# The first four expert blocks load their first weights by number from DRAM; order chosen anew, 22 first blocks

## The chip, the cores and the metric

One core of one Trainium2 chip runs one fused kernel. The metric is device time in microseconds (us), the median of the runs; less is better. Matmuls and transposes run on PE (TensorE), elementwise work on DVE (VectorE), ACT (ScalarE) and POOL (GpSimd). Loads and stores are issued by SP (SyncE), scattered and accumulating ones by POOL.

## What is computed

Two transformer layers over x of 8 batches x 256 rows x 256. Layer 0: layer norm, attention with 16 query and 4 key heads of 128 (causal softmax), then a mixture of 8 experts (2 chosen for each token) and a shared expert, computed densely. Layer 1: layer norm, linear attention, then a mixture of 16 experts with 4 chosen for each token. The part that the change touches is the last one, cut to what matters:

```python
t = xf * rsqrt(mean(xf * xf) + EPS) * norm_w            # norm_w scales the 256 input columns
vals, idx = top_k(t @ gate_w.T + gate_b, 4)
G = softmax(vals) scattered to [tokens, 16]
h = einsum('mh,eoh->emo', t, w1) + b1[:, None, :]       # w1: 16 experts, 512 x 256
a, b = minimum(h[..., ::2], 7), clip(h[..., 1::2], -7, 7)
act = a * sigmoid(1.702 * a) * (b + 1.0)
y = einsum('emi,edi->emd', act, w2) + b2[:, None, :]
return x + einsum('me,emd->md', G, y)
```

## The kernel before

**The blocks.** The tokens of layer 1 are sent, each to its four experts' lists in DRAM (`xsD`), by an indirect DMA of POOL (`f_send`, L1897). The lists are then worked off in 79 blocks of 128 rows of one expert. A table (`bi`, written by the steps `n_mm` to `n_bi`, L1739) gives each block its expert's number and its place in the lists. It is made twice: once from the first `PART` = 5 batches, for the first `FIRST` = 21 blocks, and again when all eight batches are sent, for the other 58.

**The steps of a block n.** `xb(n)` (SP, L801 to L802) loads the 128 rows. `x_t(n)` (PE, L1065, two transposes) and `x_out(n)` (ACT, L1348, one copy of 128x256) bring them into `XT`. `w_in(n)` (ACT, L1339 to L1341) reads the expert's number and copies its first weights, two pieces of 128x512, out of `W1`, where all 16 experts' weights lie, into one of the two places of `WS`, scaling by `nw` (norm_w) on the way. `h_mm(n)` (PE, L1076, 16 matmul records) multiplies; `e_a`, `e_b` (DVE, L1757, L1764), `e_tanh` (ACT, L1354), `e_g`, `e_act` (DVE, L1772, L1777) follow; `w2x(n)` (SP, L810 to L811) loads the second weights by the expert's number; `y_mm(n)` (PE, L1085), `y_out` (DVE, L1785) and `y_add` (POOL, L1926, accumulating scatter) end the block. The results of `h_mm` stand in banks 2 and 3 in turn, until `e_b` has read them.

**Where `W1` lies.** `W1` is the whole of `RA`, 16 places of 1024 columns (512 KB each), and attention uses the same memory until its end: its q, k and v weights, its output weights, the keys, values and transposed inputs. `w12(i)` (SP, L828) fills the 16 places in three steps, as attention lets go of them: i = 0 places 4, 5, 10 and 12, once batch 6 has ended and the last k and v products are done; i = 1 five places after the last `q_mm`; i = 2 the last seven (3.5 MB) after `wo(127)`, attention's last matmul. Every `w_in` waits for all of it. `WS`, `W2`, `XT` lie in `RB`, on attention's other tiles.

**The order.** Each engine runs its instructions in program order, and that order is written out by a planner (`lay_out`, `Plan`), before the kernel is built. It holds a cost for each step (`ENGINE`), a time to landing for each load (`LANDING`), and chains of steps, each chain with an allowance (`KV` ... `TURN`): at each turn it takes the step with the smallest sum of start time and allowance. Steps that could run on an idle engine but are of less hurry (the first blocks: `FILL`) have a larger allowance. SP's waits stand in the same order: a load behind a wait isn't issued before the wait ends. Behind the last of the 21 blocks the order is a fixed loop.

**Batch 7 after attention.** When `wo(127)` is done, `res(0,7)` (DVE, L1688 to L1690), the norm (L1438 to L1466), `f_mul`, `f_add` (L695, L700), `f_t` (PE, L911), `f_ht` (ACT, L1280), `s_mm` (PE, L946), `f_sig` (ACT, L1313), the choice of experts, 16 rounds of `d_mm` (PE, L962), `d_tanh` (ACT, L1301) and `d_act` (DVE, L1543 to L1545) and `d_y` (PE, L984) follow each other, then linear attention (from L1111), routing, 8 `f_send`, `f_gain`, `f_x` (POOL, L1884, L1889) and `store(7)` (SP, L832). Only then come the loads of the 22nd block and what follows.

## Time and profile before

| | us |
|---|---|
| median of 3 runs | 1042.82 (1041.34 to 1048.06) |
| the profiled execution | 1043.59 |
| its span (first to last instruction) | 1041.7 |
| PE busy | 970.5 (93% of the span) |
| DVE busy | 722.6 (69%) |
| ACT busy | 671.3 (64%) |
| POOL busy | 427.1 (41%) |
| mean granted PE clock | 0.974 of full |

An engine that is busy for most of the span is near to being the bound, but the share is a mean over stages that differ. The granted clock is that of PE: 1.0 is the upper of its two levels, 2.4 GHz, and 0.5 the lower, 1.2 GHz. The DMA share is the mean busy share of the core's 16 DMA engines.

### The profile page before, as it was taken

To read this page: it belongs to the slowest core of one execution; us is meant where nothing else is said; L and a number is where in the kernel's file an instruction comes from. 1 tells how busy PE (TensorE), PEld (TensorE's weight loads), DVE (VectorE), ACT (ScalarE), POOL (GpSimd) and SP (SyncE) were. 2 spreads that over 40 slices of the span, in tenths; PEclk is the share of its full clock that TensorE was granted. 3 is DMA by queue.
4 is the path that set the end of the run, shared out by engine and by line. 5 is a ranking of instruction groups with operands and counts; after the bars stand their busy time and mean duration, and the time that the engine had idled before them with its cause. 6 is when DMAs were issued, how large, how long until landed. Compare 5 with 4: busy or idle time off the path is not lost.

```text
span 1041.7 us, 20507 instructions
## 1 busy us (share of the span) xinstructions
PE 970.5 (93%) x6020; PEld 820.9 (79%) x6020; DVE 722.6 (69%) x2545; ACT 671.3 (64%) x1944; POOL 427.1 (41%) x450
## 2 busy tenths in 40 slices
PE   6999999999999999999999999996888799999990
PEld 4669888887988888888888888884677689999980
DVE  3564775777677678677867867776867668888870
ACT  2657786687677767757866776782735456676650
POOL 3322431342362353154236225224064555665673
PEclk9999999999999999999999999998999899999995
DMA  9928993994789210020012004057177699998954
GB/s 307 307 80 301 376 371 113 375 377 164 278 293 376 96 62 1 18 88 31 1 62 73 2 1 165 3 183 264 52 188 169 188 247 217 225 226 215 225 133 81
DMA packets 93725, 180.53 MB, mean 173 GB/s; under 512 B 9949, under 2 KB 29085, under 8 KB 92717
## 3 DMA queue, kind: packets, MB, share of 16 engines
q1 hardware_dynamic: 73467, 148.55, 43.1%
q0 software_dynamic: 18800, 30.30, 12.9%
q8 instruction: 48, 0.79, 0.3%
q10 hardware_dynamic: 1346, 0.36, 0.2%
q14 instruction: 64, 0.52, 0.2%
HBM read 77.71 MB, written 107.99 MB: 178 GB/s over the span
## 4 chain that ended last, share of the span: by engine, by line
PE 86%; DVE 4%; issue 3%; ACT 2%; DMA 2%; POOL 1%; SPq 0%; ACTq 0%; DVEq 0%; POOLq 0%; another core or an unknown queue 0%
PE bank L1076 12%; PE bank L1040 11%; PE bank L1012 10%; PE bank L1085 6%; PE bank L1030 5%; PE bank L1002 5%; PE bank L991 4%; PE bank L962 3%; PE bank L868 3%; PE bank L1031 3%; PE bank L1001 3%; PE bank L1021 3%; PE bank L877 3%; PE bank L946 2%; PE bank L984 2%
## 5 line engine op out<-in xcount | busy, mean ns | idle before, releaser
L1076 PE MATMUL bank<-RB 128*128 128x128 f32 x1264 | 157.8, 279 | 6.1 <-issue 3.8
L1076 PEld LDWEIGHTS bank<-RB 128*128 128x128 f32 x1264 | 150.6, 195 | 9.6 <-issue 4.6
L1871 POOL TENSOR_TENSOR RB<-RB 128x512 f32<-128x512 f32 x64 | 67.6, 1056 | 203.1 <-DVE RB L1650 203.1
L1040 PE MATMUL bank<-RA,RB 128*128 128x256 f32 x512 | 133.7, 383 | 1.1 <-DVE X L1690 0.8
L1341 ACT ACTIVATE RB<-RA,nw 128x512 f32 x158 | 105.5, 715 | 37.2 <-issue 16.5
L1012 PE MATMUL bank<-RA 128*128 128x256 f32 x512 | 121.2, 380 | 0.0
L1012 PEld LDWEIGHTS bank<-RA 128*128 128x128 f32 x512 | 95.2, 190 | 15.0 <-issue 2.9
L1040 PEld LDWEIGHTS bank<-RA,RB 128*128 128x128 f32 x512 | 91.0, 190 | 15.5 <-issue 4.7
L1847 POOL TENSOR_TENSOR qs<-qs,half 128x4 f32<-128x4 f32 x64 | 64.9, 1014 | 93.1 <-DVE qs L1659 79.6
L1085 PE MATMUL bank<-RB,BC 128*128 128x256 f32 x316 | 83.2, 387 | 3.3 <-DVE BC L1777 2.3
L1242 ACT ACTIVATE RB<-bank 128x256 f32<-128x256 f32 x128 | 48.7, 381 | 57.9 <-PE bank L1031 52.8
L1897 POOL DMA_INDIRECT xsD<-SC,pu x64 | 63.7, 996 | 46.7 <-DVE pu L1586 31.2
L1650 DVE COPY RB<-bank 128x512 f32<-128x512 f32 x64 | 44.2, 691 | 49.2 <-PE bank L1012 47.5
L1030 PE MATMUL bank<-RB,RA 128*128 128x256 f32 x256 | 77.0, 382 | 0.0
L1002 PE MATMUL bank<-RA 128*128 128x256 f32 x256 | 76.5, 380 | 0.0
L1223 ACT ACTIVATE RB<-bank 128x384 f32<-128x384 f32 x128 | 62.6, 491 | 20.7 <-PE bank L991 18.7
L1670 DVE CUSTOM_DVE_ANT_0 RB<-bank,cb,qs 128x128 f32<-128x128 f32 x128 | 44.1, 345 | 34.4 <-PE bank L1002 27.5
L1757 DVE TENSOR_SCALAR RB<-bank,b 128x128 f32<-128x128 f32 x158 | 48.0, 345 | 28.3 <-PE bank L1076 20.4
L1216 ACT ACTIVATE RB<-RB,sm 128x128 f32<-128x128 f32 x128 | 51.0, 398 | 20.6 <-DVE sm L1671 19.8
L991 PE MATMUL bank<-ident,RB 128*128 128x128 f32 x384 | 63.0, 273 | 1.1 <-ACT RB L1242 1.1
L1217 ACT ACTIVATE RB<-RB,sm 128x256 f32<-128x256 f32 x128 | 63.9, 500 | 0.0
L1236 ACT ACTIVATE RB<-RB,sm 128x256 f32<-128x256 f32 x128 | 63.9, 499 | 0.0
(251 smaller groups left out, 2387.3 us busy)
## 6 DMA issues: line engine op xcount, KB each, us to landing
xsD<-BC SPq DMA_DIRECT2D x17, 4232.0 KB, 33.0
RB<-in_w2b SPq DMA_DIRECT2D x79, 256.0 KB
RB<-xsD SPq DMA_DIRECT2D x62, 264.5 KB
BC<-modD SPq DMA_DIRECT2D x16, 512.0 KB, 4.2
X<-xsD SPq DMA_DIRECT2D x17, 264.5 KB, 3.4
RA<-in_w SPq DMA_DIRECT2D x2, 2048.0 KB, 8.0
RA<-in_w SPq DMA_DIRECT2D x6, 512.0 KB, 11.5
RA<-in_L_attn_Wq SPq DMA_DIRECT2D x1, 2048.0 KB, 13.8
```

What stands on the lines that cost most here:

```text
L991: m = pe.transpose(psum("p_t", u)[:, n * 128:n * 128 + 128], P[:, u % 4, n * 128:n * 128 + 128], ident[:, :])
L1002: pe.matmul(ps[:, 128:384], q[:, 128:256], k[:, 0:256], start=True, stop=True).then_inc(mine("scores", u), 1)
L1012: m = pe.matmul(psum("q_mm", p)[:, t * 256:t * 256 + 256], hT[:, b % 2, c, t * 128:t * 128 + 128], Wq[:, c, h * 128:h * 128 + 256], start= ...
L1030: pe.matmul(psum("pv", u)[:, 0:256], v[:, 0, :], PT[:, u % 2, 0:256], start=True, stop=False, skip_group_check=True)
L1040: m = pe.matmul(bank[5][:, t * 256:t * 256 + 256], OT[:, u % 2, t * 128:t * 128 + 128], Wo[:, h, :], start=(h == 0 and t == 0), stop=(h == ...
L1076: m = pe.matmul(ps[:, 128 * j:128 * j + 128], WS[:, n % 2, c, 128 * j:128 * j + 128], XT[:, n % 2, c * 128:c * 128 + 128], start=(c == 0), ...
L1085: m = pe.matmul(ps[:, 0:256], AB[:, n % 3, c * 128:c * 128 + 128], W2[:, n % 4, c, :], start=(c == 0), stop=(c == 1))
L1217: act.activation(P[:, u % 4, 128:384], P[:, u % 4, 128:384], ACT.Exp, bias=s[:, 3:4], scale=-1.0, accum_out=s[:, 5:6]).then_inc(mine("s_ex ...
L1236: act.activation(P[:, u % 4, 128:384], P[:, u % 4, 128:384], ACT.Copy, scale=s[:, 7:8]).then_inc(mine("p_norm", u), 1)
L1341: m = act.activation(WS[:, n % 2, c, :], W1[:, bass.ds(r, 1), c, :].rearrange("p a n -> p (a n)"), ACT.Copy, scale=nw[:, c:c + 1])
L1847: pool.tensor_tensor(dst, src, half[:, 0:n], ALU.pow).then_inc(sem, 1)
L1871: pool.tensor_tensor(sq, qrow, qrow, ALU.mult).then_inc(mine("q_sq", p), 1)
```

## The change

The first four blocks don't copy their weights out of `W1` any more. `w1x(n)`, n = 0 to 3, reads the expert's number of block n from the table and loads that expert's 512 KB straight from DRAM into place `PLACES[n]` (4, 5, 10, 12) of `W1`. It does so at the point at which `w12(0)` filled these places; `w12(0)` is gone. `h_mm(n)` of these four reads its weights there and waits for `w1x(n)`, not for `w_in(n)`. As these weights aren't scaled by `nw`, `x_out(n)` scales the rows instead, in two activations of 128x128. Behind `h_mm(n)`, `w12x(n)` loads the place's own expert into it (512 KB each). `w_in(n)` is there from n = 4 on and waits for `w12x(3)` beside what it waited for. `FIRST` goes from 21 to 22, so the fixed loop has 57 blocks. The planner gets costs and landing times for the new steps (5 us and 6 us), five of its ten allowances change, and chains now carry their batch, so that batch 5's chains are given 1 us more once attention has ended. With that the order of all engines is chosen anew.

```diff
-FIRST, PART = 21, 5
+FIRST, PART = 22, 5
+PLACES = 4, 5, 10, 12
+DURING, BEHIND = {5: 0, 6: 0}, {5: 1, 6: 0, 7: 0}
...
-        "SP": "clear 2.0 w12 1.0 xb 1.2 w2x 1.2 store .1 bc .1 mod_store .1 acc_zero 2.8 zrow_store 2.0",
+        "SP": "w1x .1 w12x .1 clear 2.0 w12 1.0 xb 1.2 w2x 1.2 store .1 bc .1 mod_store .1 acc_zero 2.8 zrow_store 2.0",
...
-HOP, LANDING = 0.2, {"bc": 5.0, "mod_store": 4.0, "clear": 14.0, "w12": 11.0, "xb": 3.2, "w2x": 3.5, "y_add": 4.0, "f_send": 3.0, "store": 4.0}
+HOP, LANDING = 0.2, {"w1x": 5.0, "w12x": 6.0, "bc": 5.0, "mod_store": 4.0, "clear": 14.0, "w12": 11.0, "xb": 3.2, "w2x": 3.5, "y_add": 4.0, "f_send": 3.0, "store": 4.0}
...
+    def allowance(self, c):
+        late, of = c[2].get("late", c[0]), c[4]
+        return late + (BEHIND if ("wo", NU - 1) in self.end else DURING).get(of, 0.0)
...
-    KV, QUERY, FIRSTS, SHARED, DENSE, LINEAR, LATE, UNIT, FILL, TURN = 0.04, 0, 0.1, 0.02, 0.0, 0.06, 0.1, 0.1, 0.19, -0.09
+    KV, QUERY, FIRSTS, SHARED, DENSE, LINEAR, LATE, UNIT, FILL, TURN = -0.08, 0, 0.1, 0.07, 0.0, -0.02, 0.1, 0.1, 0.24, 0.11
...
     def last_weights():
-        yield do("w12", 0, by=48, aside=True, after=[("pv", NU - 17), ("k_mm", NB - 1, 1), ("v_mm", NB - 1, 0), ("v_mm", NB - 1, 1)])
...
-        yield do("h_mm", n, bank=2 + n % 2, first=True, after=[("w_in", n)] + [("h_mm", n - 1)] * (n > 0))
+        yield do("h_mm", n, bank=2 + n % 2, first=True, after=[("w1x", n), ("wo", NU - 1)] * (n < len(PLACES)) + [("w_in", n)] * (n >= len(PLACES)) + [("h_mm", n - 1)] * (n > 0))
...
     def weights_in():
-        for n in range(FIRST):
-            yield do("w_in", n, aside=True, after=[("w12", 2), ("n_bi", 0)] + [("h_mm", n - 2)] * (n >= 2))
+        for n in range(len(PLACES), FIRST):
+            yield do("w_in", n, aside=True, after=[("w12", 2), ("w12x", len(PLACES) - 1), ("n_bi", 0)] + [("h_mm", n - 2)] * (n >= len(PLACES) + 2))
+
+    def first_weights():
+        for n in range(len(PLACES)):
+            yield do("w1x", n, slot=n, by=16, aside=True, after=[("n_bi", 0), ("pv", NU - 17), ("k_mm", NB - 1, 1), ("v_mm", NB - 1, 0), ("v_mm", NB - 1, 1)])
+
+    def weights_behind():
+        for n in range(len(PLACES)):
+            yield do("w12x", n, by=16, aside=True, after=[("h_mm", n)])
...
+            def w1x(n):
+
+                on.wait_ge(*done("n_bi", 0))
+                on.wait_ge(*done("pv", NU - 17))
+                for t in range(2):
+                    on.wait_ge(*done("k_mm", NB - 1, t))
+                    on.wait_ge(*done("v_mm", NB - 1, t))
+                r = sp.value_load(table(0, n), min_val=0, max_val=15)
+                sp.dma_start(W1[:, PLACES[n]:PLACES[n] + 1, :, :].rearrange("p e c n -> p (e c n)"),
+                             I["w1"].rearrange("p (e n) -> p e n", e=16)[:, bass.ds(r, 1), :].rearrange("p e n -> p (e n)")).then_inc(mine("w1x", n), 16)
+
+            def w12x(n):
+
+                on.wait_ge(*done("h_mm", n))
+                e = PLACES[n]
+                sp.dma_start(W1[:, e:e + 1, :, :].rearrange("p e c n -> p (e c n)"), I["w1"][:, 1024 * e:1024 * e + 1024]).then_inc(mine("w12x", n), 16)
...
-                on.wait_ge(*done("w_in", n))
+                if n < len(PLACES):
+                    w = W1[:, PLACES[n], :, :]
+                    on.wait_ge(*done("w1x", n))
+                else:
+                    w = WS[:, n % 2, :, :]
+                    on.wait_ge(*done("w_in", n))
...
-                act.activation(XT[:, n % 2, :], psum("x_out", n)[:, 0:256], ACT.Copy).then_inc(mine("x_out", n), 1)
+                if n < len(PLACES):
+                    on.wait_ge(L["small1"], 128)
+                    for c in range(2):
+                        m = act.activation(XT[:, n % 2, 128 * c:128 * c + 128], psum("x_out", n)[:, 128 * c:128 * c + 128], ACT.Copy, scale=nw[:, c:c + 1])
+                    m.then_inc(mine("x_out", n), 1)
+                else:
+                    act.activation(XT[:, n % 2, :], psum("x_out", n)[:, 0:256], ACT.Copy).then_inc(mine("x_out", n), 1)
```

## Rows read from the trace of the kernel before

**Rows 1.** The page: PE's busy share in 40 slices, in tenths.

```profile
PE   6999999999999999999999999996888799999990
```

**Rows 2.** Windows: length, busy time of each engine (instructions), granted clock, DMA share, GB/s.

```profile
core 0: us, PE busy (x) PEld busy (x) DVE busy (x) ACT busy (x) POOL busy (x), PEclk, DMA share, GB/s
...
600.00:700.00 100.00, 98.78 (x618) 83.62 (x616) 71.37 (x275) 73.22 (x226) 33.47 (x37) 1.00 0.27 91
711.00:729.00 18.00, 8.09 (x25) 4.74 (x24) 12.63 (x29) 2.48 (x6) 8.38 (x9) 0.72 0.95 341
...
711.00:845.00 134.00, 105.17 (x673) 85.79 (x672) 97.02 (x329) 63.58 (x149) 63.85 (x68) 0.90 0.66 182
```

**Rows 3.** Windows: two at the lower clock, one before; columns as in rows 2.

```profile
718.20:728.20 10.00, 3.99 (x9) 2.54 (x10) 7.10 (x15) 1.26 (x3) 2.42 (x3) 0.50 0.99 366
...
824.00:834.00 10.00, 6.21 (x22) 4.72 (x21) 4.02 (x12) 0.75 (x3) 7.93 (x8) 0.50 0.85 270
...
640.00:676.00 36.00, 35.67 (x212) 30.74 (x213) 28.11 (x122) 25.36 (x80) 12.12 (x12) 1.00 0.16 60
```

**Rows 4.** Timeline of PE: start, us, operation, idle before it and what ended it.

```profile
723.53 1.11 PE L911 MATMUL bank<-ident,SC 128*128 128x128 f32 x4 [8.38 <-DVE SC L700]
725.33 4.16 PE L946 MATMUL bank<-RB,SC 128*128 128x360 f32 x8 [0.69 <-ACT SC L1280]
729.42 2.05 PE L1076 MATMUL bank<-RB 128*128 128x128 f32 x16
```

**Rows 5.** Timeline of PE: `s_mm` of an earlier batch, at the upper clock.

```profile
570.89 2.58 PE L946 MATMUL bank<-RB,SC 128*128 128x360 f32 x8
```

**Rows 6.** Timeline of ACT: the first weight copies and their neighbours.

```profile
728.03 1.33 ACT L1341 ACTIVATE RB<-RA,nw 128x512 f32 x2 [2.27 <-DMA RA<-in_w]
729.27 0.43 ACT L1313 ACTIVATE rt<-bank 128x8 f32<-128x8 f32 x2
...
735.37 0.70 ACT L1301 ACTIVATE SC<-bank,gh 128x176 f32<-128x176 f32 x2
```

**Rows 7.** Timeline of SP's queue: loads of weights and rows.

```profile
634.76 42.18 SPq L828 DMA_DIRECT2D RA<-in_w  x5
...
712.77 2.06 SPq L828 DMA_DIRECT2D RA<-in_w  x4
716.62 4.12 SPq L811 DMA_DIRECT2D RB<-in_w2b  x4
```

**Rows 8.** DMA from 711 to 731.5 us; and L828's time to landing.

```profile
DMA packets 2008, 7.01 MB, mean 342 GB/s; under 512 B 251, under 2 KB 500, under 8 KB 1880
...
DMA to landing us min/median/max: 6.0/9.8/12.9
```

**Rows 9.** Timeline of PE: `h_mm` among batch 7's `d_mm`, then `d_mm` without.

```profile
737.32 0.46 PE L962 MATMUL bank<-RB,SC 128*128 128x352 bf16 x2
...
740.02 0.46 PE L962 MATMUL bank<-RB,SC 128*128 128x352 bf16 x2
...
744.66 0.47 PE L962 MATMUL bank<-RB,SC 128*128 128x352 bf16 x2 [0.17 <-DVE SC L1545]
...
747.04 0.47 PE L962 MATMUL bank<-RB,SC 128*128 128x352 bf16 x2 [0.95 <-DVE SC L1545]
```

**Rows 10.** The end of the transition: loads for the loop, and its first `h_mm`.

```profile
838.03 8.53 SPq L802 DMA_DIRECT2D RB<-xsD  x8
...
844.71 2.02 PE L1076 MATMUL bank<-RB 128*128 128x128 f32 x16 [0.35 <-ACT RB L1348]
```

**Rows 11.** Chain of waits in the loop: start, us, what.

```profile
873.58 1.79 PE bank L1076 x16
...
876.45 1.79 PE bank L1076 x16
```

**Rows 12.** `e_a` of a block on the timeline, and the table's writing.

```profile
734.18 0.61 DVE L1757 TENSOR_SCALAR RB<-bank,b 128x128 f32<-128x128 f32 x2 [0.88 <-issue]
...
L1739 DVE TENSOR_TENSOR bi<-bank,SC x2: 228/228/229, 644.2 to 823.9; 1x80 int32<-1x80 f32 x2
```

More of the change, by code:

```diff
@@ L111, in add, with chain @@
         self.order.append(k)
-    def chain(self, late, steps):
-        self.chains.append([late, steps, next(steps), 0.0])
+    def chain(self, late, steps, of=None):
+        self.chains.append([late, steps, next(steps), 0.0, of])
+    def allowance(self, c):
+        late, of = c[2].get("late", c[0]), c[4]
+        return late + (BEHIND if ("wo", NU - 1) in self.end else DURING).get(of, 0.0)
     def begin(self, c):
-        late, steps, ask, ready = c
+        late, steps, ask, ready, _ = c
         t = ready
@@ L146, in run @@
                 t, bank = self.begin(c)
-                late = c[2].get("late", c[0])
+                late = self.allowance(c)
                 if t is not None and (best is None or t + late < best[0]):
@@ L295, in unit @@
             yield do("res", 0, b, bank=5, last=True, after=[("bc", 0, b)])
-            p.chain(FIRSTS, ffn0(b))
+            p.chain(FIRSTS, ffn0(b), b)
     def ffn0(b):
@@ L307, in ffn0 @@
         for i in range(2):
-            p.chain(SHARED, shared(b, i))
+            p.chain(SHARED, shared(b, i), b)
         yield do("f_top", 0, b, after=[("f_sig", b, 0), ("f_sig", b, 1)])
@@ L313, in ffn0 @@
             for r in range(2):
-                p.chain(DENSE, dense(b, i, r))
+                p.chain(DENSE, dense(b, i, r), b)
             for h in range(2):
-                p.chain(DENSE, turned(b, i, h))
+                p.chain(DENSE, turned(b, i, h), b)
     def shared(b, i):
@@ L329, in shared @@
                 yield do("bc", 0, b + 3, slot=b % 3, by=16, after=[("s_x", b, 0)], aside=True)
-            p.chain(LINEAR, lin_attn(b))
+            p.chain(LINEAR, lin_attn(b), b)
     def dense(b, i, r):
@@ L366, in lin_attn @@
         yield do("res", 1, b, bank=f0, last=True)
-        p.chain(LATE, ffn1(b))
+        p.chain(LATE, ffn1(b), b)
     def ffn1(b):
@@ L391, in ffn1 @@
         yield do("f_w", 1, b)
-        p.chain(LATE, offsets(b))
+        p.chain(LATE, offsets(b), b)
         yield do("f_pos", 1, b, bank=bk, last=True, after=[("f_rank", 1, b)])
@@ L466, in lay_out @@
     p.chain(LATE, last_weights())
-    for steps in (weights_in(), weights_out(), block(0)):
+    for steps in (first_weights(), weights_behind(), weights_in(), weights_out(), block(0)):
         p.chain(FILL, steps)
@@ L811, in w2x @@
                 sp.dma_start(W2[:, n % 4, :, :].rearrange("p c n -> p (c n)"), I["w2b"][bass.ds(r, 1), :, :].rearrange("a p n -> p (a n)")).then_inc(mine("w2x", n), 16)
-            def w12(i):
-                if i == 0:
-                    on.wait_ge(*done("pv", NU - 17))
-                    for t in range(2):
-                        on.wait_ge(*done("k_mm", NB - 1, t))
-                        on.wait_ge(*done("v_mm", NB - 1, t))
-                    parts = ((4, 6), (10, 11), (12, 13))
-                elif i == 1:
+            def w1x(n):
[11 more added lines that the diff above has]
+                sp.dma_start(W1[:, e:e + 1, :, :].rearrange("p e c n -> p (e c n)"), I["w1"][:, 1024 * e:1024 * e + 1024]).then_inc(mine("w12x", n), 16)
+            def w12(i):
+                if i == 1:
                     on.wait_ge(*done("q_mm", NU // 2 - 1))
@@ L834, in _ @@
             run = {"mod_store": mod_store, "bc": bc, "acc_zero": acc_zero, "zrow_store": zrow_store,
-                   "clear": clear, "xb": xb, "w12": w12, "w2x": w2x, "store": store}
+                   "clear": clear, "xb": xb, "w1x": w1x, "w12x": w12x, "w12": w12, "w2x": w2x, "store": store}
             for stage, *key in plan.order:
@@ L1075, in h_mm @@
                     for c in range(2):
-                        m = pe.matmul(ps[:, 128 * j:128 * j + 128], WS[:, n % 2, c, 128 * j:128 * j + 128], XT[:, n % 2, c * 128:c * 128 + 128], start=(c == 0), stop=(c == 1))
+                        m = pe.matmul(ps[:, 128 * j:128 * j + 128], w[:, c, 128 * j:128 * j + 128], XT[:, n % 2, c * 128:c * 128 + 128], start=(c == 0), stop=(c == 1))
                 m.then_inc(mine("h_mm", n), 1)
@@ L1335, in w_in @@
                 on.wait_ge(*done("w12", 2))
+                on.wait_ge(*done("w12x", len(PLACES) - 1))
                 on.wait_ge(L["small1"], 128)
-                if n >= 2:
+                if n >= len(PLACES) + 2:
                     on.wait_ge(*done("h_mm", n - 2))
```

## The prediction, made before the changed kernel was run

> **What bounds the kernel now.** I read the page's slices first: PE is 9 tenths or more busy in all but a few slices, and the dip lies between slice 28 and slice 34, some 700 to 860 us [rows 1]. Then the windows: in the last 100 us of attention PE is busy for 98.78 of them, so little can be won there; from 711 us, when attention's last matmul runs, to 845 us, when the loop over the last 58 blocks takes over, PE is busy for 105.2 of 134 us and its granted clock is 0.90 [rows 2]. The transition is the place where something is to be had: 28.8 us of idle PE, and four stretches with the clock at 0.50, the lower of its two levels, of which the first and the last are shown (10 us each; the two between them have about 3 us each) [rows 3].
>
> The largest hole is the first. In 711 to 729 us PE works 8.1 us [rows 2]: it waits 8.4 us for batch 7's norm and shift on DVE, and the `f_t` and `s_mm` that follow run at the lower clock; `s_mm` takes 4.16 us [rows 4], against 2.58 us for the same 8 records of an earlier batch [rows 5]. The rows of the first blocks are there, but their weights are not: the last seven places of `W1` are only issued from 712.8 us, when attention is over [rows 7], and ACT's first weight copy waits for them until 728.0 us [rows 6]. The first `h_mm` is at 729.4 us [rows 4].
>
> The end of the transition is set by a chain, not by the amount of work: batch 7 has to go through its experts, linear attention and routing, and be sent, before the first rows of the loop can be loaded, at 838.0 us; the loop's first `h_mm` is at 844.7 us [rows 10]. From there PE is the bound, a block each 2.87 us (876.45 - 873.58) [rows 11].
>
> **The change part by part.** I make the sum against the profiled execution, 1043.6 us, which is 0.8 us above the median of the runs.
>
> *Loads ahead.* The table is written at 644.2 us [rows 12]. In place of three loads by place SP issues four by number. Its queue issued five `w12` loads in 42 us [rows 7] and the DMA engines are 0.16 busy there [rows 3], so the table reads are covered by idle time: a load by number takes 4.12 / 4 = 1.0 us of SP, one by place 2.06 / 4 = 0.5 us [rows 7], 2.6 us more in all if the cover were gone. Bytes are the same. A load of this kind lands 6.0 to 12.9 us after its issue [rows 8]; `h_mm(0)` comes tens of us later. Nothing.
>
> *The four `h_mm`.* They can now run from 711.6 us on, in the hole: 4 x 1.79 us (the length of one) [rows 11] = 7.2 us of PE work leaves the stretch after 729 us. What that is worth there is not 7.2 us but what batch 7's chain gains. Two rounds of `d_mm` with an `h_mm` between them start 2.70 us apart (740.02 - 737.32), two rounds without 2.38 us (747.04 - 744.66) [rows 9]. Three `h_mm` stood in such places. Bounds: 3 x 0.3 = 1 us by these rows, 3 x 1.79 = 5.4 us if each held the chain for its whole length. ACT helps: of the six weight copies between 728 and 744 us four go, each 1.33 us, and one of them stands right in front of `f_sig` [rows 6]. I take 2.4 us, nearer the lower end.
>
> *The clock.* In the first stretch at the lower level PE has 3.99 us of work [rows 3], all of it on batch 7's chain. If the `h_mm` keep PE at work in the hole, and the clock stays up, half of that goes: 2.0 us. Bounds 0 and 2.0; I take 2.0, as the hole of 8.4 us is what lies ahead of the fall, and three or four `h_mm` leave no part of it longer than some 3 us.
>
> *DVE's share.* `e_a` and `e_b` are 0.6 us each [rows 12]. DVE has 18 - 12.63 = 5.4 us idle in the window [rows 2], but not always where these steps come. If they push in front of batch 7's norm, the chain loses up to the 2.4 us of two blocks; if they fit into idle time, nothing. I take 1.0 us of loss. The second activation of `x_out` (some 0.3 us a block, from the 0.43 us pair at 729.27 [rows 6]) falls into ACT's idle 15.5 us of the 18 [rows 2].
>
> *One block more in the transition.* It leaves the loop: 2.87 us less, if PE has the room, and 28.8 us of idle time say so. It costs up to 2.87 us if its row load or its bank comes so late that it delays the loop's first block. I take 2.9 us of gain.
>
> *The places' own weights.* `w12x(n)` adds 4 x 512 KB = 2.1 MB behind `h_mm(n)`. Between 711 and 731.5 us the queues move 7.01 MB at 342 GB/s [rows 8], with a DMA share of 0.95 to 0.99 [rows 2, 3]: there is no room beside them, so `w12x(3)` lands up to 2.1 MB / 342 GB/s = 6.1 us after that work, near 737.6 us. `w_in(4)` can't start before. With four blocks ahead this is covered: the y half of these blocks and batch 7's experts are to be done until then. In the kernel before, the fifth `h_mm` came far later still, after the first four blocks' y half. What stands behind `w_in(4)` on ACT isn't covered; that is the first rival. The Trainium skill says in "DMA: Bandwidth & Descriptors", section "Issuing engines are not separate DMA queues", that transfers issued by SP, ACT and POOL all run on the same 16 DMA engines and interleave. By this rule the sends and the second weights delay `w12x` wherever it is issued. The shares of 0.95 and more agree. If it were not so, the nearest row would let it land 6.0 us after its issue, near 733 us; the sum stays the same in both cases, the first rival's chance doesn't.
>
> *The order.* New allowances move the steps everywhere. In attention PE is 0.99 busy [rows 2], and I cost it at 0, with 2 us either way. In the transition the last stretch of low clock has 6.2 us of PE's work in it [rows 3], 3.1 us to be lost or won, and the two short ones, of some 3 us each, up to 3.2 us more, by chance of order. I cost it at 0, with 5 us either way.
>
> Sum: 1043.6 - 2.4 - 2.0 + 1.0 - 2.9 = 1037.3 us for a profiled execution, and 0.8 less, **1036.5 us**, as a median.
>
> **The rivals.**
>
> *The wait moves to `w_in(4)` (slower).* ACT runs in order. If the planner, which lets `w12x` land 6 us after its issue, writes `w_in(4)` in front of batch 7's `f_sig` or first `d_tanh`, these stand behind a load that lands at 737.6 us. `f_sig` would go from 729.3 us to 737.6 + 1.33 = 738.9 us, 9.6 us later; the first `d_tanh`, from 735.4 us, 3.5 us later [rows 6]. With the first, the gains in clock and rounds are gone too: 1043.6 - 2.9 + 9.6 = 1050.3, as a median 1049.5 us. It decides once the stall is over 2.9 us with the other gains gone, or over 6.3 us with them. For it: ACT stood 2.27 us in front of just such a copy [rows 6]. Against it: four `h_mm` and their e steps are ready before, so the copy is hardly written early.
>
> *Only the extra block counts.* The chain of batch 7 doesn't move, since its own latencies and DVE set it and what goes in the first hole comes back in another: 1043.6 - 2.9 - 0.8 = 1039.9 us. For it: PE has idle time in all parts of the transition. Against: its `s_mm` at half clock is on the chain itself.
>
> *All of it counts.* The four `h_mm` were fully in the chain's way: 7.2 + 2.0 + 2.9 = 12.1 us, 1030.7 us. For it: PE's idle time after 729 us is short pieces, behind which each `h_mm` pushes the next. Against it: rows 9.
>
> *The order costs.* The hole closes, but the new order opens others, with another fall of the clock: 5 us plus the forecast's gain lost in part, 1045 us.
>
> **How the numbers follow.** Forecast 0.42 (own range 1034 to 1039), all of it 0.19, only the block 0.18, the order costs 0.12, the wait moved 0.09. 1036.5 us is that of the likeliest. The range for 8 in 10 goes from 1030 (all of it, less what attention may give) to 1046 (order costs); the wait moved and the tails stay out. Faster by over 1% means under 1032.4 us: all of it with luck and the low tail, 0.23. Slower by over 1% means over 1053.2 us: the moved wait at its worst, 0.04. The rest, 0.73, is within 1%, about what a measurement of this kernel can tell from no change.
>
> **What would show it.** Right: `h_mm` records (L1076 before) from some 713 us after the start of the span on, three or four before `s_mm`; `s_mm` in 2.6 us; clock 1.0 in the first window; the loop's first `h_mm` 3 to 4 us earlier and 57 blocks behind it. Wrong: ACT idle in front of `w_in(4)` and released by a DMA; `f_t` of batch 7 later than 12 us after attention's last `wo`; `s_mm` still above 4 us; a long wait in front of the loop's first rows.

## The result, and the profile after

The changed kernel took 1051.09 us, median of 12 runs (1046.93 to 1055.72), beside 1044.54 us for the kernel before on the same chip (12 runs, 1041.34 to 1048.06): 1.0065 times as long, 95% interval 1.0049 to 1.008. That is 0.65% slower, within 1%, and 5 us above the range given (1030 to 1046 us). The same kernel was measured twice more, always beside the kernel before. On chip 11 it took **0.9914** (0.9895 to 0.9932), on chip 7 **1.006** (1.0037 to 1.0082). So there are two results. The later runs were made on five chips, one session on each, and fall into two kinds, which I call kinds of chip; whether it is the chip or the session that decides isn't told apart by them:

| | kind A (chips 9, 11) | kind B (the first chip, whose number isn't known, and chips 7, 0, 13; the first may be one of these) |
|---|---|---|
| the kernel before, us | 1040.35, 1039.95 | 1044.54, 1044.66, 1043.29, 1042.34 |
| the changed kernel, ratio | 0.9914 | 1.0065, 1.006 |

The forecast, 1036.5 of 1042.82 us, is a ratio of 0.994. Kind A comes 0.3% below it, kind B 1.2 to 1.3% above it. The spans split like this (attention's end is the end of the last `wo`; all times read from the timeline):

| us | before, first chip | after, first chip | after, chip 11 |
|---|---|---|---|
| to attention's end | 712.7 | 715.1 | 705.9 |
| from there to batch 7's first `f_send` | 107.6 | 105.6 | 105.1 |
| from there to the loop's first `h_mm` | 24.4 | 33.4 | 26.6 |
| the loop and the end | 197.0 (58 blocks) | 195.7 (57) | 195.2 (57) |
| span | 1041.7 | 1049.8 | 1032.8 |

The two executions of the changed kernel are of one program, and differ in the first row and in the third, by 9.2 and 6.8 us. The middle of the transition, which the change was to shorten, is the same in both and 2.0 to 2.5 us shorter than before. The forecast had 6.3 us less for the profiled execution: 3.4 on batch 7's chain and 2.9 for the block. The first chip has 8.1 us more: 2.4 at attention's end, -2.0 on the chain, 9.0 at the loop's start and -1.3 in the loop.

Attention's last `wo` (L1068) in the two executions, first chip, then chip 11:

```profile
714.05 1.03 PE L1068 MATMUL bank<-RA,RB 128*128 128x256 f32 x4
```

```profile
704.90 1.03 PE L1068 MATMUL bank<-RA,RB 128*128 128x256 f32 x4
```

Windows of after, first chip; the first answers to the second row of [rows 2], the second to its third row:

```profile
core 0: us, PE busy (x) PEld busy (x) DVE busy (x) ACT busy (x) POOL busy (x), PEclk, DMA share, GB/s
...
715.10:731.00 15.90, 13.50 (x108) 12.94 (x108) 11.58 (x38) 4.69 (x13) 1.92 (x2) 1.00 0.95 368
715.10:854.10 139.00, 111.86 (x716) 92.25 (x715) 100.56 (x346) 61.80 (x148) 59.05 (x63) 0.89 0.64 178
822.00:854.00 32.00, 21.98 (x112) 18.07 (x111) 15.86 (x52) 9.07 (x19) 18.06 (x18) 0.73 0.67 179
```

The hole behind attention is filled: PE is busy for 13.5 of 15.9 us at clock 1.00, where it had 8.09 of 18 us at 0.72 [rows 2]. The transition as a whole is as idle as it was (27.1 us of 139, before 28.8 of 134), at 0.89 against 0.90. The last window shows where the idle time went: to the end, with the clock at 0.73.

PE's timeline there, which answers to [rows 4], and ACT's, which answers to [rows 6]:

```profile
714.92 1.95 PE L1109 MATMUL bank<-RB,RA 128*128 128x128 f32 x16
...
727.20 1.10 PE L1118 MATMUL bank<-RB,BC 128*128 128x256 f32 x4 [2.40 <-DMA RB<-in_w2b]
...
731.04 1.38 PE L974 MATMUL bank<-RB,SC 128*128 128x360 f32 x4
```

```profile
738.29 2.56 ACT L1375 ACTIVATE RB<-RA,nw 128x512 f32 x4 [0.59 <-issue]
740.96 0.70 ACT L1334 ACTIVATE SC<-bank,gh 128x176 f32<-128x176 f32 x2
```

`h_mm` (L1109) starts 0.2 us before attention's matmuls have drained. `s_mm` (L974) has its full clock (all 8 records in 2.59 us), but starts at 731.0, 16.0 us after attention's end, where it was 12.6 us (725.33 - 712.74): linear attention of batch 6 and four blocks' PE work stand before it, and a wait of 2.40 us of `y_mm(0)` (L1118) for its second weights. `w_in(4)` (L1375) does stand in front of the first `d_tanh` (L1334), for 2.56 us, but waits for no load.

The loop's start, SP and PE, which answers to [rows 10]:

```profile
845.69 0.34 SPq L828 DMA_DIRECT2D RB<-in_w2b  x1
846.07 0.43 SPq L860 DMA_DIRECT2D out<-X  x1
847.65 7.85 SPq L819 DMA_DIRECT2D RB<-xsD  x8
...
854.10 2.02 PE L1109 MATMUL bank<-RB 128*128 128x128 f32 x16 [0.35 <-ACT RB L1388]
```

`store(7)` (L860) waits behind `w2x(21)` (L828), and this for `y_mm(17)`, which is late. `f_x` of batch 7 had ended at 836.7 us, and the loop's rows could have been loaded from there.

### The profile page after: what moved, and what is told of

Same layout as the page of the kernel before. It is cut to its first block, busy times and chain, and to the rows that moved or that the text cites. A ratio compares the mean times of both kernels' runs of the same rounds, so it can differ in the third digit from the quotient of the medians.

```text
span 1049.8 us, 20509 instructions
## 1 busy us (share of the span) xinstructions
PE 974.0 (93%) x6020; PEld 823.9 (78%) x6020; DVE 722.2 (69%) x2545; ACT 670.0 (64%) x1940; POOL 426.5 (41%) x450
## 4 chain that ended last, share of the span: by engine, by line
PE 83%; DVE 4%; issue 3%; DMA 3%; ACT 2%; POOL 1%; another core or an unknown queue 1%; SPq 1%; DVEq 0%; ACTq 0%; POOLq 0%
PE bank L1109 11%; PE bank L1068 10%; PE bank L1040 10%; PE bank L1118 5%; PE bank L1030 5%; PE bank L1058 5%; PE bank L1019 4%; PE bank L990 3%; PE bank L1029 3%; PE bank L1059 3%; PE bank L896 3%; PE bank L1049 3%; PE bank L905 3%; PE bank L1012 2%; PE bank L974 2%
## 5 line engine op out<-in xcount | busy, mean ns | idle before, releaser
L1911 POOL TENSOR_TENSOR RB<-RB 128x512 f32<-128x512 f32 x64 | 66.9, 1046 | 237.5 <-DVE RB L1690 236.7
L1109 PE MATMUL bank<-RB 128*128 128x128 f32 x1200 | 151.3, 281 | 1.5 <-ACT RB L1388 1.3
L1109 PEld LDWEIGHTS bank<-RB 128*128 128x128 f32 x1200 | 145.0, 197 | 3.6 <-ACT RB L1388 1.7
L1068 PE MATMUL bank<-RA,RB 128*128 128x256 f32 x512 | 133.7, 384 | 3.0 <-ACT RB L1275 2.9
L1375 ACT ACTIVATE RB<-RA,nw 128x512 f32 x150 | 100.0, 714 | 56.9 <-issue 17.7
L1068 PEld LDWEIGHTS bank<-RA,RB 128*128 128x128 f32 x512 | 92.0, 191 | 16.9 <-ACT RB L1275 4.0
L1118 PE MATMUL bank<-RB,BC 128*128 128x256 f32 x316 | 84.3, 391 | 12.1 <-DVE BC L1817 7.3
L1118 PEld LDWEIGHTS bank<-RB,BC 128*128 128x128 f32 x316 | 55.1, 194 | 20.0 <-DVE BC L1817 9.8
L1334 ACT ACTIVATE SC<-bank,gh 128x176 f32<-128x176 f32 x128 | 49.3, 404 | 24.8 <-PE bank L990 21.5
```

The lines of the kernel that those rows point to most:

```text
L1068: m = pe.matmul(bank[5][:, t * 256:t * 256 + 256], OT[:, u % 2, t * 128:t * 128 + 128], Wo[:, h, :], start=(h == 0 and t == 0), stop=(h == ...
L1109: m = pe.matmul(ps[:, 128 * j:128 * j + 128], w[:, c, 128 * j:128 * j + 128], XT[:, n % 2, c * 128:c * 128 + 128], start=(c == 0), stop=(c ...
L1118: m = pe.matmul(ps[:, 0:256], AB[:, n % 3, c * 128:c * 128 + 128], W2[:, n % 4, c, :], start=(c == 0), stop=(c == 1))
L1375: m = act.activation(WS[:, n % 2, c, :], W1[:, bass.ds(r, 1), c, :].rearrange("p a n -> p (a n)"), ACT.Copy, scale=nw[:, c:c + 1])
L1911: pool.tensor_tensor(sq, qrow, qrow, ALU.mult).then_inc(mine("q_sq", p), 1)
```

## Late signals of PE: what sets the two kinds apart

On chips of kind B the timeline has waits whose releaser isn't seen: the profile calls it remote. In the changed kernel on the first chip each ends with a signal of PE (a semaphore counted up) that is on record 1.9 to 3.5 us behind the end of the last matmul that gives it. ACT in the changed kernel, first chip:

```profile
640.92 0.38 ACT L1275 ACTIVATE RB<-bank 128x256 f32<-128x256 f32 x1 [4.91 <-remote]
...
695.71 0.49 ACT L1256 ACTIVATE RB<-bank 128x384 f32<-128x384 f32 x1 [1.06 <-remote]
...
782.52 1.33 ACT L1375 ACTIVATE RB<-RA,nw 128x512 f32 x2 [3.53 <-remote]
...
835.84 1.33 ACT L1375 ACTIVATE RB<-RA,nw 128x512 f32 x2 [11.72 <-remote]
```

The same first and last instruction on chip 11:

```profile
637.65 0.39 ACT L1275 ACTIVATE RB<-bank 128x256 f32<-128x256 f32 x1 [3.05 <-PE bank L1059]
...
818.61 1.33 ACT L1375 ACTIVATE RB<-RA,nw 128x512 f32 x2 [4.11 <-PE bank L1118]
```

The eight profiles taken on chips 9 and 11, of seven kernels, have not one such wait. The other profiles all have them: the kernel before 2 or 4, 7.6 and 9.6 us in sum over the engines; the changed kernel 7 or 8, 30 to 32 us. In the changed kernel they stand at the same seven instructions on the first chip and on chip 7, five of them with the same length within 0.4 us (4.91 and 4.97 us for the first); with 21 blocks on chip 13 six of the seven come again (4.79 us). They end in POOL's bursts of eight sends or behind them, most within 2 us, the last at 835.8 us 5 us behind. In the changed kernel these are at 632 to 644 us (batch 4), 688.6 to 698.5 (batch 5), 771 to 782 (batch 6) and 820.7 to 830.7 (batch 7). The kernel before has the largest of its own there too, and the profile before showed it, though I didn't read it:

```profile
830.40 0.38 ACT L1348 ACTIVATE RB<-bank 128x256 f32<-128x256 f32 x1 [6.33 <-remote]
```

The trace's records of the semaphores say it without the waits. In the eight profiles of kind A all of PE's counts that can be set beside a matmul (1,265 in each) come within 0.02 us of its recorded end. In each of the twelve of kind B 10 to 24 come 0.5 us or more behind it, up to 4.1 and 4.6 us in the changed kernel and 6.3 us in the kernel with the sends moved (below). Except at the very end of some profiles, where counts before them are missing, DVE's are at most 0.06 us late on either kind.

What differs between the kernels is what a burst falls on. Before, batch 5's sends run from 706 to 715 us, across attention's end, where PE soon has little to do. The new order puts them inside attention (POOL, then PE, first chip):

```profile
688.59 1.06 POOL L1937 DMA_INDIRECT xsD<-SC,pu  x1 [2.68 <-DVE pu L1626]
...
697.57 0.96 POOL L1937 DMA_INDIRECT xsD<-SC,pu  x1 [0.31 <-issue]
```

```profile
694.71 1.13 PE L1068 MATMUL bank<-RA,RB 128*128 128x256 f32 x4 [0.56 <-ACT RB L1275]
...
698.28 0.55 PE L1019 MATMUL bank<-ident,RB 128*128 128x128 f32 x3 [1.11 <-issue]
...
701.50 2.07 PE L1068 MATMUL bank<-RA,RB 128*128 128x256 f32 x4 [2.37 <-ACT RB L1275]
```

```profile
692.60:699.50 6.90, 4.78 (x32) 3.43 (x30) 1.65 (x6) 3.44 (x11) 4.71 (x5) 1.00 0.57 221
699.50:706.30 6.80, 4.80 (x17) 3.75 (x18) 0.91 (x3) 4.08 (x12) 0.00 (x0) 0.50 0.05 17
```

PE, which is 0.99 busy in attention [rows 2], has three gaps within 7 us, 4.0 us in sum. Its granted clock falls to 0.50 at 699.5 us, at the start of the third gap (699.1 to 701.5 us), and stays there for 6.8 us; in the 6.9 us before, PE had worked 4.8. On chip 7 it was 13.7 us from 699.9 us. Laid record by record beside chip 11, the first chip is 2.7 us behind at 641.6 us, 3.5 at 694.7 and 9.1 at 706.5; then the lag stays within a microsecond or two until it grows again, from 10.7 us at 828.0 to 17.5 at 838.7, behind the last burst. Of the 17.0 us between the two executions some 14 are made in and behind bursts of sends: 1.4 at batch 4's, 5.6 at batch 5's, 6.8 at batch 7's.

## The experiments

Each number is a ratio to the kernel before on the same chip, with its 95% interval. Chip 9 first.

**The changed kernel with 21 first blocks.**

```diff
-FIRST, PART = 22, 5
+FIRST, PART = 21, 5
```

> The changed kernel with 21 first blocks in place of 22; all else (loads by number, new allowances) as in the changed one, the order chosen by the planner again. If the 22nd block is what costs (its steps stand in front of store(7) and of the loop's loads on SP), this comes out at or under the time of the kernel before, 1037 to 1045 us, and the loads of the loop start within 2 us of store(7)'s data, at 836 to 838 us. If the order or the loads by number cost, it stays at 1049 to 1053 us.

0.9919 (0.9898 to 0.994), 1032.79 of 1040.35 us, below both ranges that I expected. The forecast's ratio came in here, with all of the change but one block. Its mechanism didn't: attention ends at 707.1 us, which the forecast had at no gain, and the runs below show that batch 7's chain gains nothing from the loads. That the number fits on kind A is luck.

**The loads by number alone**: the changed kernel with 21 blocks, the old allowances and nothing for batch 5 behind attention.

```diff
-FIRST, PART = 22, 5
+FIRST, PART = 21, 5
...
-DURING, BEHIND = {5: 0, 6: 0}, {5: 1, 6: 0, 7: 0}
+DURING, BEHIND = {5: 0, 6: 0}, {5: 0, 6: 0, 7: 0}
...
-    ... = -0.08, 0, 0.1, 0.07, 0.0, -0.02, 0.1, 0.1, 0.24, 0.11
+    ... = 0.04, 0, 0.1, 0.02, 0.0, 0.06, 0.1, 0.1, 0.19, -0.09
```

> The loads by number alone: allowances as in the kernel before, 21 first blocks. If the loads by number do what the forecast says, 1038 to 1042 us (4 us less than before) with three or four h_mm in the first 16 us after attention. If they cost something themselves (2.1 MB more, w_in(4) in front of batch 7's d_tanh), 1046 to 1052 us.

1.0062 (1.0045 to 1.0079): slower by itself. Its PE timeline says why:

```profile
723.50 1.11 PE L939 MATMUL bank<-ident,SC 128*128 128x128 f32 x4 [4.12 <-DVE SC L717]
727.53 2.04 PE L1118 MATMUL bank<-RB,BC 128*128 128x256 f32 x4 [2.92 <-DMA RB<-in_w2b]
729.36 4.49 PE L974 MATMUL bank<-RB,SC 128*128 128x360 f32 x8
```

Three `h_mm` go into the hole, but the y half of block 0 now comes in front of `s_mm` and waits 2.92 us for its second weights, which are in the queues with the last 3.5 MB. `s_mm` runs at the lower clock as before, 4 us later, and attention's end to the first send is 113.1 us, not 107.6 (107.3 in the kernel before with 22 blocks, on the same chip).

**The new order alone**: the kernel before, with the new allowances and the 1 us of batch 5.

```diff
-    ... = 0.04, 0, 0.1, 0.02, 0.0, 0.06, 0.1, 0.1, 0.19, -0.09
+    ... = -0.08, 0, 0.1, 0.07, 0.0, -0.02, 0.1, 0.1, 0.24, 0.11
...
+        return late + (1.0 if of == 5 and ("wo", NU - 1) in self.end else 0.0)
```

> The new allowances alone (with batch 5's 1 us), weights loaded as in the kernel before, 21 first blocks. If the order is what costs (batch 6's linear attention is still to do when attention ends), 1048 to 1054 us, and attention's last matmul runs 2 us later than in the kernel before, near 714 us. If it doesn't, 1042 to 1047 us.

1.0002 (0.9987 to 1.0016), a little under both ranges. Neither part gains anything alone; together they gain 0.8%. Against the sum of the parts (+0.6 + 0.0) that is 1.4% for the pair. Where it comes from shows beside the first run (the first of batch 7's sends, and the loop's first `h_mm`), here:

```profile
810.66 1.00 POOL L1902 DMA_INDIRECT xsD<-SC,pu  x1 [0.59 <-DVE pu L1591]
...
845.52 2.02 PE L1081 MATMUL bank<-RB 128*128 128x128 f32 x16 [0.35 <-ACT RB L1353]
```

and with the loads by number (21 blocks, the same chip):

```profile
811.15 1.01 POOL L1937 DMA_INDIRECT xsD<-SC,pu  x1 [2.23 <-DVE pu L1626]
...
834.49 3.17 PE L1109 MATMUL bank<-RB 128*128 128x128 f32 x16
```

| us | new order alone | with the loads by number |
|---|---|---|
| attention's end | 706.3 | 707.1 |
| from there to the first send | 104.3 | 104.1 |
| from there to the loop's first `h_mm` | 34.9 | 23.3 |
| first blocks whose `h_mm` is still to do at the first send | 6 | 3 |

The order alone gains in attention and on batch 7's chain, and loses it again at the loop's start, where six of the first blocks are still to do. The loads by number give nothing on the chain; they let blocks run earlier and give 11.6 us at the loop's start. With 22 blocks on chip 11 it is the same: 105.0 and 105.1 us, then 37.7 and 26.6 us.

**22 first blocks alone**, in the kernel before.

```diff
-FIRST, PART = 21, 5
+FIRST, PART = 22, 5
```

> The kernel before with 22 first blocks and nothing else. If the 22nd block's steps in front of the loop's loads cost, 1046 to 1052 us; if the block fits into the transition's idle time, 1040 to 1043 us, 2.9 us less than with 21.

0.9978 (0.9962 to 0.9995), 2.4 us, where the sum had 2.9.

Then chip 11.

**The changed kernel itself, unedited, and once more with 21 blocks.**

> The changed kernel once more, beside its twin with 21 first blocks on one chip. The two have the same order on all engines up to the last first blocks (some 815 us), yet the profiles differ by 8 us at attention's end. If that is of the chip and of the single execution, attention ends here at 706 to 709 us and the ratio to the kernel before is 1.000 to 1.008; the stretch from batch 7's first f_send to the loop's first h_mm (33.4 us in the first profile) tells what the 22nd block costs by itself: still 31 us or more by the theory that the last first blocks are late, 24 to 27 us by the theory that the first profile was a bad execution. The latter gives 0.99 for the ratio.

> The changed kernel with 21 first blocks again, on the same chip as the one with 22. If 21 against 22 first blocks is the whole difference, 0.990 to 0.994 of the kernel before, as in the first measurement, with f_send to the loop's first h_mm in 23 to 24 us. If the first measurement was luck, 1.00.

0.9914 (0.9895 to 0.9932) and 0.9927 (0.991 to 0.9944). With the first two parts of the change the 22nd block adds too little to be told from nothing.

**`w2x(21)` moved behind `store(7)` and the loop's first rows.**

```diff
+    late = ("w2x", FIRST - 1)
+    p.order.remove(late)
+    p.order.insert(p.order.index(("w2x", FIRST)), late)
```

> The changed kernel, 22 first blocks, with one step moved on SP: w2x(21), which waits for y_mm(17), stands behind store(7) and the eight row loads of the loop, not in front of them. If SP's queue holds the loop, the loads start at f_x(7)'s end (836.7 us by the first profile, not 847.7) and the kernel gains 5 to 9 us against the changed one. If PE is late by itself, with the last first blocks' h_mm and y_mm still in front of the loop's, the loads start early but the kernel gains under 2 us.

0.9998 (0.9983 to 1.0013): 0.8% lost beside the changed kernel, where I had expected a gain either way. The store is issued 1.9 us earlier (826.32 us), but PE's order isn't changed, and there `y_mm(21)` stands before the loop's first `h_mm`:

```profile
841.27 2.05 PE L1121 MATMUL bank<-RB,BC 128*128 128x256 f32 x4 [9.44 <-DMA RB<-in_w2b]
```

The wait in front of the store is the cheaper of the two. The stretch from the first send to the loop's first `h_mm` is 34.2 us, not 26.6.

**The new order with the old weights and 22 blocks**: the kernel of the new order alone, with `FIRST` = 22.

> New allowances and 22 first blocks, weights loaded as in the kernel before (no loads by number). With 21 first blocks this order ran at 1.000 of the kernel before. If the 22nd block costs only where the fill is late, it costs here too, as the fill starts at 720 us: 1.004 to 1.010. If it is worth its 2.9 us as in the kernel before's order, 0.997.

1.0007 (0.9993 to 1.0022), neither of the two expected. The 22nd block gives 2.4 us in the old order and nothing in the new one.

Chip 7, kind B.

**The kernel before against itself, and the changed kernel for the third time.**

> The kernel before itself, timed against itself. If the ratio of the first measurement (1.0065) and of the second (0.9914) for the same changed kernel differ by the conditions of the chip, this one still has to give 1.000 within its interval, some 0.15% either way; a ratio off by more than 0.3% would say that the comparison itself is not as narrow as its interval. Its profile gives the milestones of the kernel before on this chip (on the first: attention's last matmul at 712.7 us, the loop's first h_mm at 844.7 us).

> The changed kernel for the third time. Theory A (the first measurement was made under conditions in which PE's signals come late while POOL sends, and those are rare): 0.991, as the second time. Theory B (it is a matter of the chip, and chips differ): anything between 0.991 and 1.007, and a profile that shows in which stretch it lies: attention's end at 706 or 715 us, the stretch from the last send to the loop's first h_mm 26 or 33 us. Theory C (pure chance of an execution): both values among the single times of this one run.

0.9991 (0.9979 to 1.0004) and 1.006 (1.0037 to 1.0082). The comparison is as narrow as it says, and the first result comes again with all its late signals. Theory C falls: of 6 single times here none is below 1047.5 us, of 6 on chip 11 none above 1034.6.

**`w12x` with a sixteenth of its bytes.** Fifteen sixteenths of each place's own weights are left out, so later blocks of these experts compute with wrong ones.

```diff
-sp.dma_start(W1[:, e:e + 1, :, :]..., I["w1"][:, 1024 * e:1024 * e + 1024])
+sp.dma_start(W1[:, e:e + 1, 0:1, 0:64]..., I["w1"][:, 1024 * e:1024 * e + 64])
```

> The changed kernel in its own order, but w12x loads 128x64 numbers a place, not 128x1024, so three of the four places keep the wrong expert's weights and their blocks' results are wrong: 2.0 MB less move in the first 20 us after attention. If the added bytes delay w2x(0) and w_in(4), as the working of the prediction had it (up to 6.1 us at w_in(4)), it is 1 to 3 us faster than the changed kernel beside it (0.997 to 0.999 of it). If they are covered, as the sum took it: the same, within 0.1%.

1.0049 (1.0028 to 1.007), 0.999 of the changed kernel beside it, with intervals that overlap. The medians are 2.6 us apart, the ratios 1.1 us: the added 2.1 MB cost 1 to 3 us or nothing.

**`w2x(0)` issued ahead of the last seven places.**

```diff
+    p.order.remove(("w2x", 0))
+    p.order.insert(p.order.index(("w12", 2)), ("w2x", 0))
```

> The changed kernel with one step of SP's queue moved: w2x(0) is issued ahead of the last seven places of W1 and not behind them, so that y_mm(0), which stood 2.4 us on PE in the profile of the changed kernel, finds its weights. If that wait is on batch 7's chain (f_t and s_mm are behind y_mm(0) on PE), attention's end to s_mm is 2 to 2.4 us shorter than in the changed kernel's run of the same job (17.5 us on the chip of the second measurement) and the time 0.998 of it. If DVE's norm sets s_mm anyway, it is the same.

1.0071 (1.005 to 1.0092), no gain. `s_mm` does start 13.3 us after attention's end and not 17.5, but the first send comes 108.6 us after it, not 105.7. An earlier `s_mm` was given back on the way; where, I haven't traced.

Chip 0, kind B.

**Batch 5's sends behind attention.**

```diff
+    sends = [k for k in p.order if k[0] == "f_send" and k[2] == 5]
+    for k in sends:
+        p.order.remove(k)
+    at = p.order.index(("f_add", 0, NB - 1)) + 1
+    p.order[at:at] = sends
```

> The changed kernel with one group moved: POOL issues the eight f_send of batch 5 behind f_add(0,7), some 10 us after attention's last matmul, and not inside attention's last 20 us. Chips differ so far: on two of them (before at 1040 us) the changed kernel takes 0.991, on one and in the first measurement (before at 1044.6 us) 1.006, and there PE's granted clock falls at 700 us, behind these sends, for 7 to 14 us. Theory A (on such a chip PE's signals come late during a burst of sends, the idle time that this makes lets the clock fall, and the changed order has put one burst where PE is otherwise busy without a gap): on such a chip attention's end comes back from 713 to 718 us towards 707 to 710 us and the ratio falls from 1.006 to 0.998 to 1.002; on the other kind of chip 0.991 to 0.995, as nothing is to be won there. Theory B (the sends have no part in it): the ratio stays 1.006 or 0.991, and a fall of the clock near 700 us stays on the first kind.

1.0047 (1.0033 to 1.006), above the 0.998 to 1.002 of theory A and below the 1.006 of theory B. The mechanism shows as theory A has it, the gain mostly doesn't. Attention ends at 707.9 us, the late signal at 695 and the fall of the clock at 700 us are gone, and a late signal stands behind the sends' new place (POOL, then DVE and ACT):

```profile
711.88 1.06 POOL L1942 DMA_INDIRECT xsD<-SC,pu  x1 [0.17 <-issue]
...
720.84 0.96 POOL L1942 DMA_INDIRECT xsD<-SC,pu  x1 [0.30 <-issue]
```

```profile
723.36 0.56 DVE L1850 TENSOR_TENSOR SC<-bank,mask 128x384 f32<-128x384 f32 x1 [5.99 <-remote]
```

```profile
723.42 0.60 ACT L1318 ACTIVATE SC<-bank 128x512 f32<-128x512 f32 x1 [5.19 <-remote]
```

Nearly all of the 7.2 us won (715.1 to 707.9) is lost again: the way from attention's end to the first send is 112.5 us, not 105.6. The counts for which DVE and ACT wait there come 6.3 and 6.0 us behind the ends of their matmuls. ACT's is that of batch 7's own `f_t`, so the late signal now stands on its chain.

**The new order alone, and the loads alone, once more.**

> The kernel of the allowances alone, once more. It has the changed order up to attention's end, its sends of batch 5 with it, and not the loads by number. Theory A: on a chip of the slower kind it loses what the changed kernel loses before attention's end, some 5 to 8 us, and goes from 1.000 to 1.005 or more; on the other kind 1.000 again. Theory B: 1.000 on either.

> The kernel of the loads by number alone, once more. It has the order of before up to attention's end, with the sends of batch 5 at 706 to 715 us, in the hole. Theory A: on a chip of the slower kind it loses no more than the kernel before, so 1.006 again, as on the other kind. Theory B (the loads by number themselves make the changed kernel's loss on such a chip): over 1.012.

1.0143 (1.0116 to 1.017) and 1.011 (1.0087 to 1.0132). The new order, worth 1.0002 on kind A, costs 1.4% on kind B: attention ends at 716.5 us, and the first send to the loop is 41.1 us. Windows of its last stretch of attention, to the last `wo`: chip 0, then chip 9.

```profile
694.00:716.50 22.50, 18.91 (x84) 13.88 (x82) 5.10 (x15) 10.16 (x27) 5.74 (x6) 0.77 0.23 84
```

```profile
692.00:706.30 14.30, 13.31 (x82) 10.52 (x80) 5.23 (x15) 8.97 (x25) 6.09 (x7) 1.00 0.36 139
```

84 and 82 matmuls in 22.5 and in 14.3 us. With the sends moved, and with the changed kernel on the first chip, for comparison:

```profile
695.00:708.00 13.00, 12.02 (x75) 9.76 (x74) 4.55 (x14) 8.16 (x23) 2.89 (x3) 1.00 0.20 62
```

```profile
695.70:715.00 19.30, 15.52 (x81) 12.20 (x80) 5.26 (x15) 10.38 (x29) 5.12 (x6) 0.82 0.26 89
```

The loads alone I expected at 1.006 on either kind; that was wrong by 0.5%. This kernel has two late signals that chip 9 doesn't have, 7.03 us on ACT at 716.7 and 6.67 us on DVE at 764.8 us, behind batch 5's and 6's sends. So the order is the larger part of the loss on kind B, not the whole.

Chip 13, kind B.

**Batches 5 to 7 send 256 bytes a row, not 2116.** They go to a memory of their own, so the rows of these batches are missing from the lists.

```diff
-pool.indirect_dma_start(xsD[:, :], ..., route(1)["src"][:, i, 0:ROW], None)
+pool.indirect_dma_start(xsD[:, :] if b < 5 else xsE[:, :], ..., route(1)["src"][:, i, 0:ROW if b < 5 else 64], None)
```

> The changed kernel, in its own order, but the sends of batches 5 to 7 write 256 bytes a row and not 2116, into a memory of their own, so the rows of these batches don't reach the lists and the result of their blocks is wrong; number and place of the sends are the same. If late signals of PE come from the bytes of the sends, the waits of an unseen releaser behind batches 5, 6 and 7 (1.1, 2 to 3.5 and 3 to 12 us in the changed kernel) are gone on a chip of the slower kind, the clock doesn't fall at 700 us and attention ends at 706 to 709 us; that behind batch 4 (4.9 us) stays. If they come from the number of packets or of signals, all stay. On a chip of the other kind there are none to begin with, and it tells nothing.

1.0065 (1.0044 to 1.0087). The waits stay, but for the one behind batch 6:

```profile
694.26 0.49 ACT L1257 ACTIVATE RB<-bank 128x384 f32<-128x384 f32 x1 [1.05 <-remote]
...
833.90 0.72 ACT L1376 ACTIVATE RB<-RA,nw 128x512 f32 x1 [11.59 <-remote]
```

With an eighth of the bytes the waits are 1.05 and 11.6 us, as with all of them, the clock falls at 698.4 us for 6.8 us, and attention ends at 713.8 us. It isn't the bytes. Whether it is the number of packets or of signals wasn't tried.

**21 blocks in the changed kernel, and 22 in the kernel before, once more.**

> The changed kernel with 21 first blocks, once more: 0.992 and 0.993 on two chips. On a chip of the slower kind 1.003 to 1.008 like the changed kernel, if the 22nd block has no part in the difference between chips; 0.992 on the other kind.

> The kernel before with 22 first blocks alone, once more: 0.998 on a chip of the faster kind. It has the order of before up to the last first blocks, and so loses on a chip of the slower kind what the kernel before loses there: 0.997 to 0.999 on either kind. If the late signals behind the last sends fall on another step of the loop's start, up to 1.005.

1.0082 (1.0064 to 1.0101) and 1.0006 (0.9994 to 1.0018), so the 22nd block has no part in the difference between the kinds. No version tried beats the kernel before on kind B. On both kinds together the safe one is the kernel before, with 21 or 22 blocks; on kind A the changed kernel is 0.9% faster.

## Why the prediction was wrong, by its steps

*Loads ahead: nothing.* Held. `h_mm(0)` to `h_mm(2)` wait for no weights in the profile after, `h_mm(3)` comes at 729.3 us.

*Batch 7's chain: 2.4 + 2.0 - 1.0 = 3.4 us.* Attention's end to the first send: 107.6 before, 105.6, 105.1 and 105.7 us in three profiles after. 1.9 to 2.5 us came, for another reason. The clock and the hole are as forecast, but `s_mm` is 3.4 us later by attention's end, not earlier; what was gained was gained behind it. In the old order the loads lose 5.5 us on this way, and in the new one they change it by 0.2 us (104.3 and 104.1) and by 0.1 us with 22 blocks; two executions with them are up to 2 us apart. The order alone has the gain: 103.5 to 105.0 us in three profiles, 107.1 to 107.6 in the four of the old order without the loads. My sum gave it to the loads and 0 to the order; the runs give it to the order. What the loads gave, 11 to 12 us at the loop's start beside the new order without them, stands in no term of the sum.

*One block more: 2.9 us.* 2.4 us in the old order on kind A, 0 on kind B, 1.4 us and not to be told from nothing in the changed kernel. The reason is the bound that I named, up to 2.87 us if the block delays the loop: on kind A, send to loop is 26.6 us with it and 22.5 to 23.3 without. The loop, one block shorter, took 1.3 us less.

*The order: 0, with 2 us either way in attention and 5 in the transition.* This is the step that failed, in size and in mechanism. In attention I took PE's 0.99 as a sign that little could change [rows 2]. The order gained there on kind A and lost on kind B: the runs with the new order alone show both. The end comes on kind A at 705.9 to 707.1 us, 710.2 and 711.6 in two kernels with the old order, and on kind B at 713.4 to 718.4 us in seven profiles, beside 711.2 to 712.7 in four with the old one. With the sends moved out of it, it is 707.9 us on kind B too. In the transition the last stretch cost 9.0 us (33.4 - 24.4). Of this 6.8 us are there on kind B and not on chip 11 (26.6 us), and they come behind the last burst with its late signals; that these make all of it is argued, no run took them away there. The other 2.2 us go with the 22nd block, which brings the stretch to 26.6 us in the old order on chip 9 too. The rival *the order costs* named this outcome ("opens others, with another fall of the clock"), with 1045 us and 0.12; it was 6 us short.

*The wait moved.* Right as a kind, wrong in place: not `w_in(4)`, which waited for no load, but `y_mm(0)`, for `w2x(0)`, 2.40 us on PE itself. The rule that I weighed, of the Trainium skill's page "DMA: Bandwidth & Descriptors", section "Issuing engines are not separate DMA queues", says that transfers share 16 engines whoever issues them. The second weights stand among the last 3.5 MB, and the DMA share there is 0.95, which fits. Both are SP's own loads, so this wait doesn't show what transfers of another issuer would do.

*The range* took in what the cover of each step could cost in the trace of one chip. That the same program takes 1.9% longer on some chips than on others, where the kernel before takes 0.45%, was outside it. The trace had one row that could have warned me, the 6.33 us of an unseen releaser at the end of the last burst of sends.

**What stays open.** Why chips or sessions differ; whether packets or signals of the sends do it; and whether the recording of the profile has a part. The profiles of kind B hold 9,763 to 10,103 updates of semaphores, those of kind A 11,444 to 11,540, for programs of one size. So updates are missing there; in the kernel before with 22 blocks 1,631 are, of which 1,417 are of landing transfers. It isn't why the releaser of the waits above isn't seen: the first two of the changed kernel wait on semaphores whose counts are all on record, 1.9 and 2.3 us behind the ends of their matmuls.

## What to carry to other kernels

A wait whose releaser the trace doesn't name, for an instruction that by its record has ended, belongs in the sum: look which traffic runs just before it, and whether the change moves that traffic into a stretch without slack. Price an order that is chosen anew by where its bursts of sends fall and by how much work it leaves behind the last of them, not by the busy share of the engine: here one burst inside a full stretch went with 5.6 us lost, and moved out of it onto the chain behind, with 6.9 us lost there. When two parts of a change are priced in one sum, run each alone: here each was worth nothing or less, and the pair 0.8%. Measure a change of under 1% on more than one chip before believing its sign.

## What the runs showed of the hardware

- The same program: 1031.33 us on chip 11 and 1050.55 us on chip 7, with the kernel before at 1039.95 and 1044.66 us. The sign of the change depends on the chip or on the session. Durations of single instructions agree (`h_mm` 280 ns a record on both, the weight copy 714 ns); only waits differ.
- On the first chip and on chips 7, 0 and 13 PE's signals come late in or behind a burst of eight indirect sends, by up to 6.3 us; on chips 9 and 11 by no more than 0.02 us. In the same program they are late at the same instructions each time (waits of 4.91 and 4.97 us). Moving the burst moves the late signal; an eighth of its bytes leaves it.
- Gaps of 0.56 and 1.11 us in an otherwise full stretch of PE came before a fall of the granted clock to 0.50 for 6.8 us, which began 0.4 us into a third gap of 2.37 us; on chip 7, in the same stretch, it was 0.50 for 13.7 us.
